# Both f16 halves of the transposed x1 written by VectorE, with new step lists and rewritten first and last batches

## The reference

```
x  = x + layernorm( attention( layernorm(x) ) )
x  = x + layernorm( ffn( layernorm(x) ) )

attention(h): q = h Wq;  lat = (h Wk + h Wv) W_down
              k = lat W_up_k;  v = lat W_up_v;  16 heads of 16
              scores = clip(q k^T / 16) * exp(-1e-4 |i - j|)
              softmax over keys, times v, times Wo
ffn(h):       xh = h H            (H: Hadamard matrix / 16)
              s = max|row of xh| / 7;  xq = round(xh / s) * s
              out = xq (ternary weights * their row scale)^T
```

## Time and profile before

| what | value |
|---|---|
| device time, median of 3 runs | 1462.9 us (1462.45 to 1466.45) |
| the profiled execution, device time | 1464.74 us |
| its span | 1462.9 us, so 1.84 us lie around it |
| TensorE busy | 1352.3 us, 92% |
| VectorE busy | 1195.8 us, 82% |
| ScalarE busy | 1154.1 us, 79% |
| GpSimd busy | 734.9 us, 50% |
| mean granted TensorE clock | 0.975 of full speed |

### The profile page before, as it was taken

The page is one execution under the profiler, slowest core; times in us unless marked ns, Lnnn a source line. Parts: engine busy times, 40 slices in busy tenths (PEclk is TensorE's granted clock), DMA queues, the critical chain, the costliest instruction groups (busy, mean ns, idle before and its releaser), DMA issues.

```text
span 1462.9 us, 35910 instructions
## 1 busy us (share of the span) xinstructions
PE 1352.3 (92%) x12330; PEld 601.3 (41%) x12330; DVE 1195.8 (82%) x2732; ACT 1154.1 (79%) x1252; POOL 734.9 (50%) x1060
## 2 busy tenths in 40 slices
PE   5789999999999999999999999999999999999852
PEld 3334444444444444444444444444444444444331
DVE  6657888889889888988888898888888888988643
ACT  0677888888888888888888888888888888888822
POOL 2324455555455465545545564554556455554333
PEclk9999999999999999999999999999999999999975
DMA  5445564565556556555654555555455456545320
GB/s 180 144 137 163 180 195 153 176 196 149 169 188 195 164 160 196 161 170 175 194 173 156 191 170 167 169 195 186 152 185 182 152 174 193 194 136 179 108 61 30
DMA packets 174541, 241.45 MB, mean 165 GB/s; under 512 B 28320, under 2 KB 145184, under 8 KB 174496
## 3 DMA queue, kind: packets, MB, share of 16 engines
q1 hardware_dynamic: 140160, 206.78, 44.9%
q10 hardware_dynamic: 34336, 34.08, 7.4%
HBM read 154.80 MB, written 69.21 MB: 153 GB/s over the span
## 4 chain that ended last, share of the span: by engine, by line
PE 57%; DVE 17%; POOL 13%; issue 6%; ACT 4%; DMA 1%; SPq 1%; DVEq 0%; POOLq 0%; ACTq 0%
PE heads_ps L644 20%; PE scores_ps L631 12%; PE misc_ps L565 8%; PE misc_ps L533 5%; PE misc_ps L584 4%; POOL y_sb L955 4%; DVE diagonal L1163 3%; PE misc_ps L544 3%; DVE ln_stats L1021 3%; DVE x L1101 3%; POOL q_hl L964 3%; ACT probs L839 2%; PE misc_ps L555 2%; POOL ln_rstd L929 2%; POOL ln_root L929 2%
## 5 line engine op out<-in xcount | busy, mean ns | idle before, releaser
L839 ACT ACTIVATE probs<-scores_ps 128x1024 f32<-128x1024 f32 x768 | 765.5, 1029 | 231.6 <-PE scores_ps L631 231.4
L644 PE MATMUL heads_ps<-probs,v_sb 128*32 128x512 f32 x4096 | 525.5, 603 | 2.3 <-DVE heads L1064 1.8
L1163 DVE TENSOR_TENSOR diagonal<-scores_ps,comp 128x1024 f32<-128x1024 f32 x256 | 311.1, 1215 | 79.8 <-PE scores_ps L631 79.8
L631 PE MATMUL scores_ps<-q_rep,k_rep 64*128 64x128 f16 (+2 forms) x5120 | 329.9, 252 | 30.1 <-ACT probs L839 19.8
L631 PEld LDWEIGHTS scores_ps<-q_rep,k_rep 64*128 64x128 f16 x5120 | 164.6, 94 | 391.1 <-ACT probs L839 196.2
L922 POOL TENSOR_TENSOR ln_neg_mean<-zero,ln_moments 128x4 f32<-128x4 f32 x128 | 38.7, 302 | 421.1 <-DVE ln_moments L1029 421.0
L846 ACT ACTIVATE probs<-diagonal 128x2048 f32<-128x2048 f32 x128 | 246.8, 1928 | 0.0
L964 POOL TENSOR_TENSOR k_hl<-weighted,k_hl 128x768 f16<-128x768 f32 x64 | 105.8, 1653 | 123.9 <-DVE k_hl L1082 123.9
L644 PEld LDWEIGHTS heads_ps<-probs,v_sb 128*32 128x32 f32 x4096 | 91.1, 108 | 168.6 <-issue 164.1
L1075 DVE SCALAR_TENSOR_TENSOR weighted<-misc_ps,edges 128x384 f32<-128x384 f32 x256 | 128.7, 544 | 37.4 <-PE misc_ps L544 30.9
L565 PE MATMUL misc_ps<-wo,heads_c 128*128 128x256 f32 x512 | 129.4, 396 | 7.4 <-POOL heads_c L969 7.4
(11 more groups left out here) (110 smaller groups left out, 1530.3 us busy)
## 6 DMA issues: line engine op xcount, KB each, us to landing
q_rep<-q_scratch SPq DMA_DIRECT2D x128, 384.0 KB, 4.0
k_rep<-k_scratch SPq DMA_DIRECT2D x256, 192.0 KB, 4.4
q_scratch<-q_hl SPq DMA_DIRECT2D x64, 384.0 KB, 2.9
k_scratch<-k_hl SPq DMA_DIRECT2D x64, 384.0 KB, 3.8
x_in<-in_L_attn_x_dram ACTq DMA_DIRECT2D x32, 512.0 KB, 4.1
heads_c<-heads SPq DMA_DIRECT2D x256, 64.0 KB, 2.3
x_res<-in_L_attn_x_dram ACTq DMA_DIRECT2D x32, 512.0 KB, 5.7
den_spread<-den_scratch SPq DMA_DIRECT2D x256, 64.0 KB, 2.3
```

Of the source, the lines that this page charges most:

```text
L631: ins = mm(scores_ps[:, place + par, at:at + n * P], k_rep[rows, pair, kv_, k_cols], q_rep[rows, pair, qv_, q_cols], start=True, stop=True)
L644: ins = mm(heads_ps[W32 * g:W32 * (g + 1), :], v_sb[:, b.slot, kt, at:at + W32], probs[:, quad % 2, g, kt, :], start=(kt == 0), stop=(kt = ...
L839: nc.scalar.activation(flat[:, :, at:at + S], scores_ps[:, place:place + 2, :], ACT.Exp, scale=EXP_SCALE).then_inc(off_probs, 1)
L1163: v.tensor_tensor(diagonal[:, quad % 2, 2 * two:2 * two + 2, :], scores_ps[:, place:place + 2, :], comp[:].rearrange("p t n -> p (t n)").u ...
```

## The change

1. **x1.** ScalarE's `x1T_take` is gone. `x1_low` on VectorE now makes both halves of a bank: a copy from PSUM to f16, a wait for it, and the subtraction.
2. **The step lists.** All five tables are new. On TensorE the first pv of an iteration moves between steps 10 and 11, x1T is split over steps 12 and 13 with a pv behind it, and qintT stands behind a pv. On GpSimd `heads_normalize` moves ahead of the split of k's second half, and the split of q's second half ahead of the next layernorm. On SyncE a store of k stands ahead of `spread_den`, and `pack_den` behind four copies of heads.
3. **Closing.** The tables no longer run in iterations 32 to 34. Each engine has a list of its own for them, with seven PSUM banks in place of three; the last batch passes in two halves of 256 tokens from `heads_normalize` on.
4. **Opening.** SyncE waits for its first four loads before it issues the next; ScalarE waits for x before it loads the ffn and q weights. `ternary_weights` and `diagonal_tables` move ahead in VectorE's program, `path_choice` moves ahead of the last q, and the second batch's x_apply ahead of the last split.

The diff, cut to its core:

```diff
 TENSOR_STEPS = {
...
-    7: [("pv_end", 3, 3), ("lat", 0, 0)], 9: [("q", 0, 0), ("q", 0, 1)], 11: [("pv", 0, 0)], 13: [("x1T", 0, 0), ("x1T", 1, 0)],
-    15: [("pv", 0, 1), ("k", 0, 0), ("pv", 0, 2), ("k", 1, 0), ("pv", 0, 3)], 17: [("v", 0, 0), ("xh", 0, 0)],
+    7: [("pv_end", 3, 3), ("lat", 0, 0)], 9: [("q", 0, 0), ("q", 0, 1)], 10: [("pv", 0, 0)], 12: [("x1T", 0, 0)],
+    13: [("x1T", 1, 0), ("pv", 0, 1)], 15: [("k", 0, 0), ("pv", 0, 2), ("k", 1, 0), ("pv", 0, 3)], 17: [("v", 0, 0), ("xh", 0, 0)],
...
-POOL_STEPS = ["x1_apply", "rstd4", ("q", 0), ("k", 0), ("k", 1), "add_out", "heads_normalize", "x_apply", "rstd2", ("q", 1)]
+POOL_STEPS = ["x1_apply", "rstd4", ("q", 0), ("k", 0), "heads_normalize", ("k", 1), "add_out", ("q", 1), "x_apply", "rstd2"]
...
+TENSOR_CLOSING = [
+    ("z", 3, None, 0, 0), ("pv_end", 1, None, 3, 0), ("pv_end", 1, None, 3, 1), ("pv_end", 1, None, 3, 2), ("pv_end", 1, None, 3, 3),
+    ("z", 3, None, 1, 0), ("x1T", 2, None, 0, 0), ("x1T", 2, None, 1, 0), ("xh", 2, None, 0, 0), ("xh", 2, None, 1, 0),
+    ("y", 1, 0, 0, 0), ("y", 1, 0, 0, 1), ("y", 1, 1, 1, 0), ("y", 1, 1, 1, 1), ("qintT", 2, None, 0, 0), ("z", 2, None, 0, 0),
...
-            for i in range(B - 2, B + 3):
+            for i in range(B - 2, B):
                 one(i)
+        def closing(back, half=None):
+            return Batch(0, B - back, 2, half, back)
...
             for dst, src in first:
                 sp.dma_start(dst, src).then_inc(first_loaded, 16)
+            sp.wait_ge(first_loaded, 16 * FIRST)
...
-            def x1T_take(b, part):
-                act.wait_ge(in_psum["x1T"], part_count("x1T", b, part))
-                nc.scalar.activation(x1_hl[:, 0, part, :], misc_ps[:, BANK["x1T", part], :], ACT.Copy).then_inc(x1_high, 1)
...
             def opening_batch(b):
                 load_x(b, 0)
+                act.wait_ge(x_loaded, 16)
+                nc.scalar.dma_start(wf, ffn_weight.rearrange("(c p) n -> p c n", p=P)).then_inc(ffn_loaded, 16)
                 nc.scalar.dma_start(wq[:], Wq.rearrange("(c p) n -> p c n", p=P)).then_inc(second_loaded, 16)
-                nc.scalar.dma_start(wf, ffn_weight.rearrange("(c p) n -> p c n", p=P)).then_inc(rest_loaded, 16)
...
             def x1_low(b, part):
+                dve.wait_ge(in_psum["x1T"], part_count("x1T", b, part))
+                if b.half is None:
+                    high, low, src = x1_hl[:, 0, part, :], x1_hl[:, 1, part, :], whole(bank_of("x1T", part, b))
+                else:
+                    high, low, src = x1_hl[:, 0, :, b.columns], x1_hl[:, 1, :, b.columns], tokens(bank_of("x1T", part, b))
+                v.tensor_copy(high, src).then_inc(x1_high, 1)
                 dve.wait_ge(x1_high, part_count("x1T", b, part))
-                v.tensor_tensor(x1_hl[:, 1, part, :], misc_ps[:, BANK["x1T", part], :], x1_hl[:, 0, part, :], ALU.subtract)\
-                    .then_inc(taken["x1T"], 1)
+                v.tensor_tensor(low, src, high, ALU.subtract).then_inc(taken["x1T"], 1)
```

More of the change, by code:

```diff
@@ L29, with __init__ @@
 class Batch:
-    def __init__(self, loop, offset, buffers):
-        self.loop, self.offset, self.buffers = loop, offset, buffers
+    def __init__(self, loop, offset, buffers, half=None, back=None):
+        self.loop, self.offset, self.buffers, self.half, self.back = loop, offset, buffers, half, back
+        self.rows = slice(0, 4) if half is None else slice(2 * half, 2 * half + 2)
+        self.columns = slice(128 * self.rows.start, 128 * self.rows.stop)
+        self.tiles = range(self.rows.start, self.rows.stop)
+        self.last_part = 1 if half is None else half
         self.number = buffers * loop + offset
@@ L79 @@
 }
 VECTOR_STEPS = {
[L81 to L85, removed]
-}
@@ L111, with closing_banks, bank_of @@
 BANK = bank_table()
+def closing_banks():
+    table = {}
+    for stage, back, half, part, _ in TENSOR_CLOSING:
+        key = stage, (half or 0) if stage == "qintT" else part, back
+        if stage in PARTS and key not in table:
+            table[key] = len(table) % CLOSING_BANKS
+    return table
+CLOSING_BANKS = 7
+CLOSING_BANK = closing_banks()
+def bank_of(stage, part, b):
+    return BANK[stage, part] if b.back is None else CLOSING_BANK[stage, part, b.back]
 GENERAL_ORDER = {when: [step for name in names for step in ORDER_ALL if step[0] == name]
@@ L474, in fast_path @@
                 run_pipeline(sp, iteration)
-                sp.wait_ge(out_stored, OPEN + 16 * B)
+                for step, back, half, *part in SYNC_CLOSING:
+                    steps[step](closing(back, half), *part)
+                sp.wait_ge(out_stored, OPEN + 16 * (B + 1))
             def general_path():
@@ L588, in qintT_stage @@
             def qintT_stage(b, part, piece):
-                pe.wait_ge(qint_ready, b.number + 1)
-                bank = claim("qintT", part, b)
-                for t in range(T):
+                pe.wait_ge(qint_ready, b.done)
+                bank = claim("qintT", b.half or 0, b)
+                for t in b.tiles:
                     for c in range(DC):
@@ L665, in enter_loop @@
             def enter_loop(loop, b):
-                for held in holder:
+                for held in holder[:3]:
                     await_taken(*held)
@@ L744, in fast_path @@
                 run_pipeline(pe, iteration, enter_loop)
+                for stage, back, half, part, piece in TENSOR_CLOSING:
+                    stages[stage](closing(back, half), part, piece)
             def general_path():
@@ L875, in fast_path @@
                 run_pipeline(act, iteration)
+                for stage, back, half, part in SCALAR_CLOSING:
+                    takes[stage](closing(back, half), part)
             def general_path():
@@ L904, in general_path @@
                         nc.scalar.activation(heads[:, a, :], heads_ps[:], ACT.Copy).then_inc(g_taken, 1)
-                    for step, parts in (("x1T", 2), ("round_x", T), ("qintT", 1), ("z_apply", T)):
+                    for step, parts in (("round_x", T), ("qintT", 1), ("z_apply", T)):
                         for part in range(parts):
@@ L996, in fast_path @@
                 run_pipeline(pool, iteration)
+                for step, back, half in POOL_CLOSING:
+                    steps[step](closing(back, half))
             def general_path():
@@ L1258, in fast_path @@
                 run_pipeline(dve, iteration)
+                for step, back, half, *part in VECTOR_CLOSING:
+                    steps[step](closing(back, half), *part)
             def general_path():
```

209 lines of the change are left out of this document (126 added, 83 removed), and 7 rows, old and new, of tables (TENSOR_CLOSING, TENSOR_STEPS, VECTOR_CLOSING).

## The result

| | before | after |
|---|---|---|
| device time, median of 4 runs | 1463.03 us | 1483.07 us (1479.91 to 1485.24) |
| ratio, 95% interval | | 1.013 [1.0106, 1.0155] |
| profiled execution, span | 1464.74, 1462.9 us | 1482.49, 1480.7 us |
| period of the loop | 42.45 us | 44.01 us |

What follows compares the result with a forecast made beforehand. It took the loop as bound by VectorE's chain from step 0 to k and otherwise by TensorE, the ends by latency. 1464.7 + 10 (loop) - 7 (opening) - 12 (closing) = 1455.7, less 1.8 for the runs' median: 1454 us, range 1438 to 1469.

Steps and rivals of the forecast that it cites:

- The stretch from step 0 to k is bound by VectorE's chain: Loop: VectorE's gapless work, with two 0.68 us copies added, sets when TensorE's k starts: +0.23 us an iteration.
- rival A: Loop gets no longer, by a 0.42 us copy or a vanished exponentials wait: -0.3 to +0.1 us an iteration; chance 0.25.
- The new places of pv and x1T only decide where TensorE's idle time lies: TensorE's list ahead of k: the moves shift idle time, not when k starts; given no value.
- heads_normalize starts at 574.6 as against 574.49: GpSimd in the steady loop: it waits for denominators, taken as landing 6.6 us after the first spreading DMA is issued.
- The cast of q's weighting is held by the k split: VectorE beside GpSimd: held 0.3 to 0.6 us, just borne by step 24's diagonal; 0.1 us put on this and quantization together.
- Quantization: VectorE meets add_out, q_int ready at 582.0 as TensorE wants it; 0.1 us together with the cast, bounds 0 and 0.9.
- Rival B: GpSimd meeting: later denominators make quantization wait out add_out, TensorE stands at qintT; 1.13 us an iteration, 1477 us; chance 0.12.
- Rival C: Half of the GpSimd meeting: 0.5 us at qintT and step 26, 1466 us, no change; chance 0.16.
- signs of being wrong: Period under 42.4 us, qintT wait over 0.3 us, cast mean near 0.4, or first scores after 38 us.
- signs of being right: Period 42.6 to 42.9, gapless VectorE, cast 0.68, k within 0.1, first scores 34 to 36, closing about 53 us.
- The opening: Start to first scores: first loads alone 1.5 us, gaps filled 6.2, later loads -0.7; -7 us, bounds -9 and -3.
- The closing: Last heads to end: earlier first moments 4.1 us, halves 7.5, smaller last store 0.5; -12 us, bounds -15 and -8.

Runs made afterwards that it cites:

- before_copies_dve: The kernel before with only x1's two copies moved from ScalarE to VectorE: 1478.63 us, 1.0096.
- before_new_pool: The kernel before with only GpSimd's new order: 1501.07 us, 1.0255.
- denominators_later: The changed kernel with SyncE's store of q ahead of the spreading of the denominators: 1453.57 us, 0.9921.
- closing_whole: `act_high_add_last` with the last batch's two halves merged in all five closing lists: 1447.35 us, 0.9886.
- act_high_add_last: The changed kernel with ScalarE making x1's high halves in the loop and add_out behind the split of q's second half on GpSimd: 1436.84 us, 0.9826.
- denominators_earlier: The changed kernel with SyncE's spreading of the denominators ahead of the store of k: 1474.85 us, 1.0073.

## Why the prediction was wrong

- **"The stretch from step 0 to k is bound by VectorE's chain", +0.23.** Right: k came 0.20 later, the copy took 680 ns by the groups of lines and not the 0.42 us of rival A, which is the time of the copy from 16 bit to 16 bit, and the loop without the collision is 0.13 us longer than before (42.58 against 42.45). "The new places of pv and x1T only decide where TensorE's idle time lies" was wrong, and hidden in that net figure: the sum took x1T to be ready when VectorE comes to it, and in the old places it isn't (`before_copies_dve`). All five lists together give 0.27 (42.18 with ScalarE's copies), the copies cost 0.40.
- **"heads_normalize starts at 574.6 as against 574.49".** This term failed first. It rests on 6.6 us from the first spreading DMA to the landing, taken from the third iteration because in the steady loop add_out stood ahead and hid the landing. Measured in the steady loop: 577.18 - 571.47 = 5.7 us, in `before_new_pool` 5.6. From the iteration's first diagonal I had 574.6 - 546.34 = 28.26 us; it became 27.40. The trace of before could have bounded it. In its iteration 5 the first spreading DMA was issued late, and heads_normalize still started straight behind add_out, so the denominators were in after 277.33 - 271.79 = 5.54 us at most:

```profile
271.79 3.59 SPq L421 DMA_DIRECT2D den_spread<-den_scratch  x8
274.99 2.38 POOL L973 TENSOR_TENSOR out_sb<-out_sb,x 128x1024 f32<-128x1024 f32 x1 [2.64 <-ACT out_sb L807]
277.33 2.35 POOL L969 TENSOR_TENSOR heads_c<-heads_c,den_spread 128x1024 f32<-128x1024 f32 x1
```

`denominators_later` is the forecast's own case: heads_normalize at 28.27 us, the cast first, period 42.66, where my +0.33 gave 42.77. With this one term right the loop comes within 0.11 us of the sum.
- **"The cast of q's weighting is held by the k split ... by 0.3 to 0.6 us, which the diagonal of step 24 just bears".** The step that made the forecast wrong. With heads_normalize 0.9 us earlier the k split is over and add_out has begun when the cast comes up. The cast is held 1.88 us, of which about 0.5 is borne and 1.34 to 1.43 reach TensorE. My bounds of 0 to 0.9 were drawn for quantization; I had not asked what else GpSimd could be doing at the cast. By my own times the k split ends, and add_out begins, at 574.6 + 2.35 + 1.65 = 578.6, with the cast only some 0.5 us ahead of it: less than the 0.9 by which the landing was off. (The 581.4 for add_out's end was mis-added as well: 578.6 + 2.38 is 581.0. Nothing hung on it.)
- **Quantization** wasn't held (677 ns), y and qintT didn't wait. Rival B had the mechanism and nearly the size, 1.13 us of the 1.56 measured, with a chance of 0.12, but the wrong place, and the wrong direction: it was to decide from a *later* landing on, and a later landing is what removes the wait (`denominators_later`). Rival C named step 26, at 0.5 us together with qintT. Of the signs of being wrong that I had listed none came, and only the period, 44.01, fell outside the signs of being right: the wait showed at a place where I had not told the reader to look.
- **The loop**: +37.8 us where I had +10, nearly all of it in the 24 iterations 6 to 29. This is the whole error; the ends together came out 1 us better than forecast.
- **The opening**: -6.1 against -7, first scores at 35.37 (34 to 36). Right in sum; of its terms only the 1.5 us of the first loads was tested by itself.
- **The closing**: -13.9 against -12. The halves gave 10.3 us of it by the spans (106.2 us from the last iteration's first diagonal to the end in `closing_whole`, 95.9 in `act_high_add_last`), not 7.5 plus 0.5; order and earlier statistics 3.8 as against 4.1. GpSimd's 1/sqrt took 0.69 to 0.82 on half the columns (six times, 128x2) instead of 1.01 to 1.02, the gain I had left out; how much of what the halves gave beyond my sum that is, no run shows.

## What to carry to other kernels

When GpSimd's order changes, list for each of its long instructions what VectorE could start beside it, over the whole uncertainty of the wait ahead of it; here the cast took 2.44 us beside add_out and 0.56 alone, and a lead of 0.35 us decided over 36 us. A time that a queue hides in the steady loop must not be filled in from a warm-up iteration without trying both sides: here 6.6 us were filled in, and 5.7 measured. The cure cost nothing here: exchange two neighbours, or cut the long GpSimd instruction into pieces.

## What the hardware did that I had not expected

**In these traces who began first kept the other out, both ways.** The cast (SBUF to SBUF, 0.56 us alone) took 2.44 us when add_out began 0.35 us earlier, and add_out 2.69 in place of 2.36 when the cast began first, by 0.66 us in iteration 5 and by 0.50 in `denominators_later`; the cast ended 0.42 to 0.43 us after add_out whether add_out led by 0.04 (`denominators_earlier`, iteration 3), 0.27 (`before_new_pool`), 0.35 or 0.80 us (`denominators_earlier`), so its length is what was left of add_out and these 0.4 us. Even a row scale of 128x2 in the closing took 1.67 us instead of 0.17, beside add_out at 1463.93:

```profile
1464.63 1.67 DVE L1214 TENSOR_SCALAR xscale<-absmax 128x2 f32<-128x2 f32 x1
```

That a cast coming up behind add_out waits for its end is read from these times alone; what holds it there no run shows.

**x1's cast out of PSUM took 0.68 us beside GpSimd too.** x1's copy ran at 564.07 in 0.68 us beside a GpSimd split:

```profile
564.12 1.65 POOL L1043 TENSOR_TENSOR q_hl<-weighted,q_hl 128x768 f16<-128x768 f32 x1
```

Neither got longer: the copy's mean over the loop is 0.68, the longest of all 64 took 0.69, and the split took 1.65 at 579.51 with no copy beside it. Nor was everything within SBUF held: four statistics of x_in took 1.39 us beside heads_normalize at 577.34, and 1.40 for those of y_sb at 546.60 with GpSimd idle. In this case, then, it is the casts within SBUF, the row scale and quantization that were held by GpSimd's long instructions.

**The state of the loop.** Iterations 3 to 5 had the cast first, those from 6 to 29 add_out, and iteration 30, in which heads_normalize started 28.06 us after the first diagonal, the cast again. In iteration 5 the eight spreading DMAs took 4.54 us to issue, from iteration 6 on about 3.63. But slow issuing doesn't explain the 6.6 us on which the forecast rested: in the third iteration of before they were issued in 3.60 us, in the steady loop in 3.61. Why the denominators land later in the first iterations stays open.
